# Gated outputs in expert order: the first half through a token-order buffer, the second half added into the output array by accumulating scatters

## The reference, cut to what matters

```
logits = t @ switch_w + switch_b
route_prob = jax.nn.softmax(logits, axis=-1)
route_prob_max = jnp.max(route_prob, axis=-1)
routes = jnp.argmax(route_prob, axis=-1)
for e in range(n_experts):
    h = jax.nn.gelu(t @ w1[e] + b1[e])
    y = h @ w2[e] + b2[e]
    out = jnp.where((routes == e)[:, None], y, out)
out = out * route_prob_max[:, None]
...
x = x + jnp.tanh(g_ffn[3]) * ffn(_layernorm(x))
```

## Time and profile before

| | |
|---|---|
| median of 3 runs | 1058.42 us (1056.05 to 1059.7) |
| profiled execution | 1058.71 us, its span 1056.9 us |
| busy: TensorE | 909.0 us (86%) |
| busy: VectorE, ScalarE, GpSimd | 727.5 (69%), 633.7 (60%), 631.3 us (60%) |
| mean granted TensorE clock | 0.956 of full speed |
| chain that ended last | PE 51%, POOL 18%, DVE 11%, issue 10%, ACT 8%, DMA 2% |

### The profile page before, as it was taken

How to read it: one execution, slowest core, us unless ns; L and a number is a source line. 1 busy time by engine, 2 the same in 40 slices (tenths; PEclk the granted TensorE clock), 3 DMA queues, 4 the chain that set the end, 5 groups by cost and what they waited for, 6 DMA issues and landing times.

```text
span 1056.9 us, 21908 instructions
## 1 busy us (share of the span) xinstructions
PE 909.0 (86%) x7627; PEld 735.7 (70%) x7627; DVE 727.5 (69%) x1618; ACT 633.7 (60%) x1496; POOL 631.3 (60%) x706
## 2 busy tenths in 40 slices
PE   2788888899798998686899998999999988768993
PEld 1566666677798988455676776777777766558993
DVE  6899999373577576577799895555555568836674
ACT  2666776533565656677688775555555556444663
POOL 0466776637773373689878685444444466636753
PEclk9899999999899999998999999999999999868997
DMA  7980000001332341110000000000500000022334
GB/s 233 335 234 2 1 2 1 1 23 53 104 109 59 85 114 51 28 29 16 19 2 1 2 1 2 1 1 2 179 2 2 1 2 2 27 56 62 94 96 147
DMA packets 76846, 57.54 MB, mean 54 GB/s; under 512 B 13603, under 2 KB 69539, under 8 KB 76548
## 3 DMA queue, kind: packets, MB, share of 16 engines
q1 hardware_dynamic: 70148, 42.59, 14.3%
q0 software_dynamic: 6592, 13.58, 4.2%
HBM read 35.30 MB, written 24.08 MB: 56 GB/s over the span
## 4 chain that ended last, share of the span: by engine, by line
PE 51%; POOL 18%; DVE 11%; issue 10%; ACT 8%; DMA 2%; DVEq 0%; SPq 0%; POOLq 0%; ACTq 0%
PE psS L1209 9%; PE psO L1826 5%; PE psS L1818 5%; PE psO L1219 5%; PE psT L1763 5%; PE psS L1219 4%; PE psS L1752 3%; POOL ring L2155 3%; POOL sorted_x L1439 3%; POOL xrows L1414 3%; PE psO L1777 3%; POOL ring L847 2%; PE psO L1784 2%; ACT oTs L1925 1%; POOL sorted_z L1452 1%
## 5 line engine op out<-in xcount | busy, mean ns | idle before, releaser
L2155 POOL TENSOR_TENSOR ring<-ring,mx 128x1024 f32<-128x1024 f32 x94 | 178.3, 1904 | 104.4 <-DVE mx L2032 104.2
L1913 ACT ACTIVATE pT<-psT 128x512 f32<-128x512 f32 x192 | 114.7, 597 | 163.0 <-PE psT L1763 163.0
L1266 ACT ACTIVATE pT<-psS,b1copy 128x128 f32<-128x128 f32 x468 | 133.7, 368 | 84.2 <-PE psS L1209 84.2
L1763 PE MATMUL psT<-ident,ring 128*128 128x128 f32 x768 | 125.1, 287 | 26.8 <-POOL ring L2155 19.9
L1209 PE MATMUL psS<-ring 128*128 128x128 f32 x936 | 130.7, 285 | 13.8 <-DVE ring L1324 7.9
L1763 PEld LDWEIGHTS psT<-ident,ring 128*128 128x128 f32 x768 | 87.5, 145 | 67.6 <-issue 25.5
L1209 PEld LDWEIGHTS psS<-ring 128*128 128x128 f32 x936 | 119.5, 200 | 17.0 <-issue 8.0
L2024 DVE TENSOR_TENSOR ring<-psS,bias 128x1024 f32<-128x1024 f32 x96 | 112.6, 1215 | 10.0 <-PE psS L1752 8.3
L2032 DVE TENSOR_REDUCE mx<-ring 128x16 f32<-128x1024 f32 x96 | 112.1, 1208 | 0.0
L1321 DVE COPY ring<-w 128x512 f32 x117 | 54.4, 465 | 57.9 <-PE psO L1219 31.5
L1414 POOL DMA_INDIRECT xrows<-sorted_y,rows x64 | 61.8, 965 | 51.0 <-DMA sorted_y<-pT 33.1
(11 more groups left out here) (304 smaller groups left out, 2076.4 us busy)
## 6 DMA issues: line engine op xcount, KB each, us to landing
w<-w_dram SPq DMA_DIRECT2D x34, 256.0 KB, 5.8
sorted_x<-late SPq DMA_DIRECT2D x18, 256.0 KB, 3.6
ring<-sorted_x SPq DMA_DIRECT2D x18, 256.0 KB, 3.5
sorted_y<-pT SPq DMA_DIRECT2D x17, 256.0 KB, 2.5
sorted_z<-blank_dram SPq DMA_DIRECT2D x2, 1584.0 KB, 10.2
ring<-sorted_z SPq DMA_DIRECT2D x12, 256.0 KB
xrows<-token_y SPq DMA_DIRECT2D x8, 256.0 KB, 3.5
ctxz<-ctxz_dram SPq DMA_DIRECT2D x1, 1056.0 KB, 5.6
```

The source lines that it names most:

```text
L1266: op = nc.scalar.activation(hs[:, j % 2, f, :], psS[:, j % 2, f * P:(f + 1) * P], func, bias=b1copy[:, j % 4, f:f + 1])
L1763: mm = nc.tensor.transpose(psT[:, i * P:(i + 1) * P], ring[:, u % NS, p * P:(p + 1) * P], ident[:])
L1913: nc.scalar.activation(pT[:, u % 2, 4 * h:4 * h + 4, :].rearrange("p a q -> p (a q)"), psT[:, :], ACT.Exp).then_inc(s_pT, 1)
L2155: nc.gpsimd.tensor_tensor(rows_, rows_, mx[:, u % 4, 0:NH].rearrange("p h -> p h ()").broadcast_to([P, NH, SK]), ALU.subtract).then_inc(s_ ...
```

## The change

The weight is applied to the outputs while they are still in expert order, and the second half never goes through token_y.

- `choose` gets a sixth step, the subtraction of the maximum, which stood at the end of `place_rows`. `gates` is new work: `gates_scalar` takes tanh(z/2) instead of exp(z), and VectorE forms exp(z) = (1 + tanh(z/2)) / (1 - tanh(z/2)), sums it, inverts the sum, and writes the weight into a second column behind each row, so that it travels with the row through sorted_z. `gates` therefore moves ahead of `rank`: for the first half into stream step 44 (ScalarE's part too), for the second half in front of `outputs(0)`, with ScalarE's part after the gelu of tile 3.
- ids holds two numbers per row, token and weight (pwz). `outputs` and `output_of_one` get a second instruction, the product with pwz; TensorE waits for the first of the two (ix), GpSimd for the second (ye).
- Second half: x is stored to the output array by one 1 MB DMA right after the token numbers of the first half are loaded (`residuals_of_second`), and 23 indirect DMAs add the weighted outputs to it in DRAM (compute_op add). Padding rows go to rows of their own behind the output, whose array grows by 3072 rows.
- First half: through token_y as before, but `combine_first` is one addition per chunk, placed one group earlier, in front of groups 7, 8, 9 and 10; one 1 MB store follows.
- The second half's fetch, its 16 combining instructions, the three gate steps and the last three stores are gone.

```diff
+                step(nc.vector.tensor_tensor(pr, pr, over(m), ALU.subtract))
+                assert done[0] == LOWERED
+
+            def gates():
+
+                dve.wait_ge(s_gates[1], h + 1)
+                step(nc.vector.tensor_scalar(tmp, pr, -1.0, 1.0, ALU.mult, ALU.add))
+                step(nc.vector.reciprocal(tmp, tmp))
+                step(nc.vector.scalar_tensor_tensor(tmp, pr, 1.0, tmp, ALU.add, ALU.mult))
+                step(nc.vector.tensor_reduce(sm, tmp, AXX, ALU.add))
+                step(nc.vector.reciprocal(sm, sm))
+                dve.wait_ge(s_token, 2)
+                at = h * HT
+                for rows_, low, high in ((rows_low, 0, LOW * CH), (rows_high, LOW * CH, NT)):
+                    a, b = max(at, low), min(at + HT, high)
+                    if a < b:
+                        step(nc.vector.tensor_scalar(rows_[:, a - low:b - low, D + 1], sm[:, a - at:b - at], tg[:, LAYERS + 3:LAYERS + 4], None, ALU.mult))
...
+            nc.scalar.activation(rt3[h][:, 0], rt3[h][:, 0], ACT.Tanh, scale=0.5).then_inc(s_gates[1], 1)
...
-        def combine_last(dve, h, cc):
-            dve.wait_ge(s_yl[cc], (h + 1) * 16)
-            for t in range(h * HT + cc * CH, h * HT + (cc + 1) * CH):
-                op = nc.vector.scalar_tensor_tensor(x[:, t, :], fetched[:, t, :], pw[:, 0, t:t + 1], x[:, t, :], ALU.mult, ALU.add)
-            op.then_inc(FF[3].x.sem, 1)
+        def combine_first(dve, cc):
+            dve.wait_ge(s_yl[cc], 16)
+            chunk = slice(cc * CH, (cc + 1) * CH)
+            nc.vector.tensor_tensor(x[:, chunk, :], x[:, chunk, :], fetched[:, chunk, :], ALU.add).then_inc(FF[3].x.sem, 1)
...
-            m = n - (1 if r == 0 else 0) - NC // 2
+            m = n - 1 - NC // 2
...
-                    nc.vector.tensor_tensor(yslots[g % YS][:, 0:n * P], moe_out[r][:, s, 0:n * P], b2copy[:, s, 0:n].rearrange("p t d -> p (t d)"), ALU.add).then_inc(q.ye.sem, 1)
+                    nc.vector.tensor_tensor(y, moe_out[r][:, s, 0:n * P], b2copy[:, s, 0:n].rearrange("p t d -> p (t d)"), ALU.add).then_inc(q.ix.sem, 1)
+                    dve.wait_ge(*q.ix(g + 1))
+                    dve.wait_ge(s_ids[half], 16)
+                    rows_ = y.rearrange("p (t d) -> p t d", d=D)
+                    nc.vector.tensor_tensor(rows_, rows_, pwz[:, half, k:k + n].rearrange("p t -> p t ()").broadcast_to([P, n, D]), ALU.mult).then_inc(q.ye.sem, 1)
...
+                if r and g == 0:
+                    second_gates()
                 outputs(g)
...
                 if g % n == 0:
                     pool.wait_ge(s_ids[g // n], 16)
+                    if g:
+                        pool.wait_ge(s_out[1], 16)
...
+                    if g < n:
+                        op = nc.gpsimd.indirect_dma_start(token_y, to, y, None)
+                    else:
+                        op = nc.gpsimd.indirect_dma_start(out, to, y, None, compute_op=ALU.add)
+                    op.then_inc(s_ys[g % YS], 16)
...
                 if n == RANK_AT:
+                    gates()
                     rank()
```

More of the change, by code:

```diff
@@ L287, in build @@
         s_token, s_ids = sem("tokens_set"), [sem(f"sorted_tokens_loaded{h}") for h in range(2)]
-        s_ys, s_yl = [sem(f"outputs_scattered{k}") for k in range(YS)], [sem(f"outputs_loaded{k}") for k in range(NC // 2)]
+        s_ys = [sem(f"outputs_scattered{k}") for k in range(YS)]
+        s_yl = [sem(f"outputs_loaded{k}") for k in range(NC // 2)]
         s_tw = sem("ternary_steps")
         s_ws = sem("ternary_sum")
-        s_out = sem("out")
+        s_out = [sem("sums_stored"), sem("residuals_stored")]
         block = ctx.enter_context(nc.Block())
@@ L371, in last_moe_sync @@
                     if h and g == 3:
-                        outputs_of(0)
-            outputs_of(1)
+                        outputs_of_first()
+            sums_of_first()
+            for k in range(YS):
+                sp_.wait_ge(s_ys[k], scattered(k, 2 * n))
         @block.sync
@@ L432, in _ @@
                 last_moe_sync(sp_)
[L433 to L436, removed]
+            sp_.wait_ge(s_out[0], 16)
         def statistics(n, tile, count):
@@ L1105, in place_rows @@
                 step(nc.vector.tensor_copy(rows[:, h * HT:(h + 1) * HT], idx))
-                assert done[0] == RANKED
+                assert done[0] == RANKED[h]
                 n = LAST_HALF
@@ L1112, in place_rows @@
                 step(nc.vector.tensor_copy(expert[:, h * n:(h + 1) * n], expf[:, h * n:(h + 1) * n]))
[L1113 to L1122, removed]
+            return choose, gates, rank, place_rows
         def gates_scalar(act, h):
-            act.wait_ge(s_half[h], SHIFTED)
-            nc.scalar.activation(rt3[h][:, 0], rt3[h][:, 0], ACT.Exp).then_inc(s_gates[1], 1)
+            act.wait_ge(s_half[h], LOWERED)
+            nc.scalar.activation(rt3[h][:, 0], rt3[h][:, 0], ACT.Tanh, scale=0.5).then_inc(s_gates[1], 1)
         def shared_tensor(pe):
@@ L1281, in moe_scalar @@
                         keep_last(act)
+                    if r and j == GATES_TILE:
+                        gates_scalar(act, 1)
                     if t == 1 and g + 1 < GROUPS[r]:
@@ L1366, in moe_vector @@
                     if r:
-                        combine_last(dve, 0, g - m)
+                        combine_first(dve, g - m)
                     else:
@@ L1384, in moe_vector @@
                     rank_second()
[L1385 to L1388, removed]
         def penalties(pool):
@@ L2104, in stream_vector @@
             dve.wait_ge(s_pen, 8)
-            choose, rank, place_rows, gates = route_parts(dve, 0)
+            choose, gates, rank, place_rows = route_parts(dve, 0)
             for n in range(FIRST, NB + 4):
@@ L2142, in stream_vector @@
                     place_rows()
-                if n == NB + 3:
-                    gates()
             def take_last():
@@ L2280 @@
     head = np.arange(P) // DK % GH
-    blank = np.zeros((ROWS3, ZW), np.float32)
-    blank[:, D] = (HT * P + np.arange(ROWS3)).astype(np.int32).view(np.float32)
+    blank = np.zeros((2, ROWS3, ZW), np.float32)
+    for h in range(2):
+        blank[h, :, D] = ((h + 1) * HT * P + np.arange(ROWS3)).astype(np.int32).view(np.float32)
     data = {
@@ L2322 @@
     ins = {k: nc.dram_tensor(k + "_dram", v.shape, mybir.dt.from_np(v.dtype), kind="ExternalInput").ap() for k, v in data.items()}
[L2323 removed]
+    out = nc.dram_tensor("out_dram", (B * S + ROWS3, D), F32, kind="ExternalOutput").ap()
     sorted_x, sorted_y = (nc.dram_tensor(name, (rows, D), F32, kind="Internal").ap() for name, rows in (("sorted_x", ROWS), ("sorted_y", TOTAL[0] * P)))
     sorted_z = [nc.dram_tensor(f"sorted_z{half}", (ROWS3, ZW), F32, kind="Internal").ap() for half in range(2)]
[L2326 removed]
+    token_y = nc.dram_tensor("token_y", (HT * P + ROWS3, D), F32, kind="Internal").ap()
     build(nc, ins, out, sorted_x, sorted_y, sorted_z, token_y)
     r = run_bass_kernel_spmd(nc, [{k + "_dram": v for k, v in data.items()}], core_ids=[0])
[L2329 removed]
+    return r.results[0]["out_dram"][0:B * S].reshape(B, S, D)
```

61 lines of the change are left out of this document (36 added, 25 removed).

## The result

The changed kernel takes 1071.36 us (median of 4 runs, 1069.22 to 1073.28), the kernel before 1058.66 us beside it: a ratio of 1.0121, 95% interval 1.0096 to 1.0146. It is 12.7 us slower. The forecast was 1057.8 with a range up to 1066.

What follows compares the result with a forecast made beforehand. Bound: VectorE and GpSimd up to 964.92, then TensorE, then 14.5 us of tail. The tail saves 10.9 us, 9.6 and 0.7 are paid: span 0.6 less, median 1057.8, own range 1055.2 to 1061.6, with rivals 1053 to 1066.

Steps and rivals of the forecast that it cites:

- Steps 1 to 5: Step 44 gate 3.05 us; TensorE 1.75 late at experts' start; second gate 4.95; first-sum wait, TensorE 7.9 late; clock loss 1.7.
- third rival: Dearer clock (3.1 us lost) or ScalarE table loads, up to 2.6 us in each of two places; chance 0.1.
- step 4: VectorE waits at the first combine_first for its fetch; tile 30's up product at 1017.6, TensorE 7.9 us late.
- Step 6: Tail: adding scatter takes 0.96 us on GpSimd, last starts at 1052.7, lands in 3.2, closing 0.4, end 1056.3.
- the prediction's own signs of being wrong: Accumulating DMAs over 1.3 us apart with their data ready, or VectorE not waiting for the fetch.
- second rival: Accumulating scatter slow on GpSimd from group 9 on: end 1062.6 at 1.44 us each, 1067 at twice the work; chance 0.27.
- the sum's: Whole program: 10.9 us saved at the tail, 9.6 and 0.7 paid ahead; span 1056.3 against 1056.9.

Runs made afterwards that it cites:

- Experiment 2: Changed kernel with the first half's residual sums one group later, in front of groups 8 to 11: 1064.17 us, ratio 1.0057 to the kernel before.
- Experiment 1: Changed kernel with the second half's 23 output scatters writing in place of adding: 1065.17 us, ratio 1.0058 to the kernel before.
- Experiments 7 and 8: First half gated and combined as before, second half as changed: ratio 1.0044; the same with scatters writing in place of adding: 0.9971 on one chip, 0.9958 on another.
- Experiments 4 and 5: Kernel before without second-half fetches, gate, combining and last stores: 1050.05 us; changed kernel with a 256 KB load after its scatter waits: 1071.07 us.
- plain_second: The kernel of Experiment 1: the changed kernel with second-half scatters writing in place of adding, 1065.17 us.
- number 9: Kernel before with the first half's gate behind the weight copies and its 1 MB store before the second half's fetches: 1052.76 us, ratio 0.9956.
- store_first: Kernel before with only the first half's 1 MB store moved before the second half's fetches: 1188.64 us, ratio 0.9987, on the 1190 us chip.

## Why the prediction was wrong

Its points, with after's times corrected by 1.65 us:

| point | predicted | measured |
|---|---|---|
| first transposes | 941.45 | 942.1 |
| first up product | 943.2 | 943.9 |
| first output scatter | 960.9 | 960.8 |
| tile 30's up product | 1017.6 | 1016.9 |
| TensorE's last down product | 1049.8 | 1051.2 |
| last scatter starts | 1052.7 | 1059.2 |
| end | 1056.3 | 1068.15 |

**Steps 1 to 5 held, in mechanism and nearly in size.** The gate delays the rows by 3.5 us (3.05 predicted), and the reciprocal costed at 953 ns took 0.95 us. The wait at the first sum came where it was put, released by the fetch of xrows.

The wait was longer (6.27 us for 4) because the work around it arrived early: `outputs(6)` came 3.5 us before its forecast, since TensorE, 4.4 us late at tile 8, was only 1.5 us late at tile 28. The kernel before ran from tile 8 on at half clock, after ran tile 8 at full clock. That hid in the wait; the sum started within 0.9 us of its time.

The clock fell behind the gap: three groups of eight matmuls took 1.89 to 2.08 us in place of 1.06, so 2.6 us are lost where 1.7 were forecast. Another 1.2 us go over the last tiles, where one up product waits 0.19 us for VectorE's copies; this loss was not tried by itself. So TensorE ended 11.0 us late and not 9.6. Experiment 2 confirms the wait and the clock together, not each. No table was loaded in front of the second half's tanh, and none in step 44; of the third rival only the dearer clock came true.

Two readings in step 4 are off, without effect on the result: the 39 scatters stand 1.28 us apart on average, not 1.26, and 3.5 us isn't half of the 4.5 to 6.7 in the earlier trace rows; the fetch brought its first chunk in 2.9 us.

**Step 6 is the one that failed, in both of its terms.** It took the plain scatter's 0.96 us for the adding one, "to which it is nearest in rows and bytes"; it is 1.55, and the intervals with their data ready were 1.86 us and more; above 1.3 was one of the prediction's own signs of being wrong. The last scatter is 6.5 us late. Experiment 1 divides that: with plain scatters it starts at 1053.9, 1.2 us late, because TensorE ended later, and the adding costs the other 5.3. The second rival had this mechanism, and its price of 1 us per 0.1 us was about right: at 1.55 us it gives about 1064. Experiments 7 and 8 show the same price in another order of the work.

The other term is the 3.6 us from the last scatter to the end; it was 8.9. The landing was sized well (3.3 us for 3.2). The 0.4 us behind it was read in a kernel whose last work was SyncE's store. Behind the end of GpSimd's last scatter come 7.3 to 7.4 us, whatever the scatter does, and the kernel before hid them under its tail. Experiments 4 and 5 show it. This term, 5.3 us, was in no rival; without it the time would have come out at the upper edge of the range, 1066. No row of before shows it, but the 0.4 was carried from one engine to another with no bound on it.

So of the 10.9 us that step 6 had as saved, 5.6 remained, and the 10.3 us paid ahead of it and the 6.5 at the last scatter exceeded them. Of the sum's 11.85 us of error 5.3 are the adding, 5.3 GpSimd's end and 1.2 TensorE.

## What to carry to other kernels

Here the stretch that closes the program went with the engine that works last. When a change makes another engine the last one, the old closing time says nothing, and a kernel cut off behind that engine's last instruction measures it in one run. Price a new DMA kind by what its issuing engine does for it, and multiply by the longest unbroken run on that engine. Where two bounds lie behind each other, each repair alone shows less than it frees (9.3 us on TensorE, 7 at the end), so try them together too.

## What the hardware showed that was not expected

- GpSimd works 1.55 us on an indirect DMA of 128 rows of 512 bytes that adds, and 0.96 us on one that writes, to the same place; it lands after 3.3 us for 2.3. The software queue has 2576 packets more in after than in plain_second, 112 for each of the 23 (queue: packets, MB, share; after, then plain_second):

```profile
q0 software_dynamic: 9168, 13.58, 5.2%
...
q0 software_dynamic: 6592, 13.58, 4.1%
```
The Trainium skill's rule on reductions (Collectives: The Full Stack, cited in step 6) gave an estimate of 1.44 us; the direction agrees, and the row is 0.11 us above it.
- From the end of GpSimd's last indirect DMA to the end of the program it is 7.3 to 7.4 us, in all ten traces here that end with one. What passes in them isn't shown.
- A VectorE instruction that starts beside a GpSimd subtraction can last until that one ends: 1.24 and 1.20 us for 0.22 to 0.3. The Trainium skill has this (SBUF — State Buffer, "Who interferes with whom": in some modes VectorE and GpSimd share a pair of ports, and one blocks the other for a whole instruction), and the two rows agree with it; that the port is the cause was not tried by itself.
- After the same gap of 3.12 us in front of tile 8's up product the eight matmuls of that product took 2.04 us in the kernel before and 1.13 in number 9: a gap alone does not say whether the clock falls. In store_first, behind 3.20 us, it fell one product later.
